# Expert layer of a four-layer network: the two halves of a weight slot waited for, released and fetched apart

## The reference, cut to what matters

```
h = concatenate([pooled.transpose(1, 0, 2), ones])         # 64 experts, 4 rows, 128 + 1
h = gelu(einsum('ebd,edh->ebh', h, weight1))               # 128 (+1) -> 512
h = concatenate([h, ones])
out = einsum('ebh,eho->ebo', h, weight2)                   # 512 (+1) -> 128
```

## Time and profile before

| | |
|---|---|
| median of 3 runs | 3849.9 us (3847.41 to 3853.53) |
| the profiled execution's own time | 3838.93 us |
| its span (first to last instruction) | 3837.2 us |
| mean granted TensorE clock | 0.894 |
| instructions | 82407 |
| busy: PE, DVE, ACT, POOL | 81%, 78%, 68%, 63% of the span |
| the expert loop, 3231.06 to 3326.25 us of the span | 95.2 us, 2.5% of the span |

### The profile page before, as it was taken

One profiled execution on the slowest core, in us unless ns is written; L12 is line 12 of the kernel. 1 busy time (PEld: TensorE's weight loads), 2 busy tenths in 40 slices (PEclk: granted clock), 3 DMA queues, 4 the chain that ended last, 5 costly groups with the idle time before them and its releaser, 6 DMA issues. The chain is left out here.

```text
span 3837.2 us, 82407 instructions
## 1 busy us (share of the span) xinstructions
PE 3117.9 (81%) x29120; PEld 2153.4 (56%) x29152; DVE 2983.9 (78%) x5876; ACT 2603.1 (68%) x5243; POOL 2413.1 (63%) x2896
## 2 busy tenths in 40 slices
PE   7999589999999999999987676788848856678486
PEld 3776356666666666666665353366636534366355
DVE  3999579999999999999998467399858653278754
ACT  5888489999999999999995310267656362077562
POOL 2899588888889998888884220278755130044850
PEclk8999799999999999999999778777769867789698
DMA  3000100000000000000000523510000014500424
GB/s 94 24 24 26 52 4 13 24 24 24 24 24 24 21 17 22 24 24 24 24 18 20 134 56 113 189 29 23 7 6 1 1 25 149 183 5 1 125 52 127
DMA packets 271007, 172.54 MB, mean 45 GB/s; under 512 B 41648, under 2 KB 249976, under 8 KB 268536
## 3 DMA queue, kind: packets, MB, share of 16 engines
q1 hardware_dynamic: 270600, 167.25, 15.2%
HBM read 116.59 MB, written 50.60 MB: 44 GB/s over the span
## 5 line engine op out<-in xcount | busy, mean ns | idle before, releaser
L1246 DVE TENSOR_TENSOR_SCAN mam_hs<-mam_dA,mam_ps_b 128x1024 f32<-128x1024 f32 x512 | 1141.6, 2270 | 80.7 <-issue 43.8
L1162 ACT ACTIVATE mam_dA<-mam_dt,mam_A 128x496 f32<-128x496 f32 x1024 | 658.6, 710 | 0.4
L1018 PE MATMUL mam_ps_h<-mam_ident,mam_hs 128*128 128x128 f32 x4096 | 549.6, 277 | 60.6 <-ACT mam_hTb L1170 30.1
L1018 PEld LDWEIGHTS mam_ps_h<-mam_ident,mam_hs 128*128 128x128 f32 x4096 | 454.1, 142 | 226.3 <-issue 148.5
L1170 ACT COPY mam_hTb<-mam_ps_h 128x512 f32<-128x512 f32 x768 | 423.8, 588 | 96.5 <-PE mam_ps_h L1018 96.5
L1004 PE MATMUL mam_ps_b<-mam_DB,mam_dtxt 32*128 32x512 f32 x2048 | 292.4, 638 | 77.7 <-DVE mam_hs L1246 73.6
L1031 PEld LDWEIGHTS mam_ps_y<-mam_hTb,mam_WC 128*32 128x32 f32 x8192 | 208.9, 109 | 133.2 <-issue 124.4
L1031 PE MATMUL mam_ps_y<-mam_hTb,mam_WC 128*32 128x128 f32 x8192 | 276.7, 276 | 0.3 <-issue 0.3
L780 POOL TENSOR_TENSOR mam_cv<-mam_cv,mam_tap 128x512 f32<-128x512 f32 x180 | 239.1, 1328 | 14.1
L816 POOL TENSOR_TENSOR mam_WC<-mam_cp,mam_m 128x128 f32<-128x128 f32 x512 | 194.3, 410 | 19.9 <-POOL mam_cv L780 14.8
L1256 DVE COPY mam_hTb<-mam_ps_h 128x512 f32<-128x512 f32 x256 | 174.3, 681 | 37.8 <-PE mam_ps_h L1018 36.0
(11 more groups left out here) (742 smaller groups left out, 8236.1 us busy)
## 6 DMA issues: line engine op xcount, KB each, us to landing
moe_wg<-in_L_ffn_weight SPq DMA_DIRECT2D x32, 1024.0 KB, 8.0
rnn_xr<-x SPq DMA_DIRECT2D x23, 512.0 KB, 6.1
l1y_wh<-mode_weights SPq DMA_DIRECT2D x16, 544.0 KB, 3.7
gat_hg<-in_x SPq DMA_DIRECT2D x16, 512.0 KB, 7.2
h<-gat_out SPq DMA_DIRECT2D x32, 256.0 KB, 2.3
mam_ht<-h SPq DMA_DIRECT2D x128, 64.0 KB, 2.0
mam_hr<-h SPq DMA_DIRECT2D x128, 64.0 KB, 2.0
mam_xt<-in_x SPq DMA_DIRECT2D x128, 64.0 KB, 2.1
```

What stands on the lines that cost most here:

```text
L1018: last = pe.transpose(ps_h[n][:, q * P:(q + 1) * P], hs[:, w % 3, c:c + P], ident[:, :])
L1162: act.activation(dA[:, h, :, n, 1:], dt[:, i % 2, h, :].rearrange("p (q t) -> p q t", q=Q)[:, :, 1:], ACT.Exp, scale=A[:, h, n:n + 1]).the ...
L1246: dve.tensor_tensor_scan(hs[:, w % 3, :], dA[:, h, first:first + 2, :, :].rearrange("p q s t -> p (q s t)"), ps_b[:, 2 * (w % 2):2 * (w % ...
```

## The change

The slot gets two sets of semaphores, `win_a` for first halves and `win_b` for second halves. `weights(i)` is split into `first_weights(i)` and `second_weights(i)`. `hidden(i)` waits for `win_a` alone; `output(i)` has a wait for `win_b` in front. From group 4 on, the first half of group i is issued once `hidden(i - 4)` is done (`hid`), and the second half of group i once `output(i - 4)` is done (`out_done`) as before; SP's stream issues them in the order first 4, first 5, first 6, second 4, first 7, second 5, and so on up to first 15, second 13, second 14, second 15. The transfers themselves are the same 32, of the same sizes; there are four semaphores more.

```
-            def weights(i):
-                wa, wb = expert_weights(i)
-                sp.dma_start(wa, w1v[i][0:P]).then_inc(win[i % 4], 16)
-                sp.dma_start(wb..., w2v[i]...).then_inc(win[i % 4], 16)
+            def first_weights(i):
+                sp.dma_start(expert_weights(i)[0], w1v[i][0:P]).then_inc(win_a[i % 4], 16)
+            def second_weights(i):
+                sp.dma_start(expert_weights(i)[1]..., w2v[i]...).then_inc(win_b[i % 4], 16)
...
-            for i in range(4, NG):
-                sp.wait_ge(out_done, i - 3)
-                weights(i)
+            for i in range(4, NG + 2):
+                if i < NG:
+                    sp.wait_ge(hid, i - 3)
+                    first_weights(i)
+                if i >= 6:
+                    sp.wait_ge(out_done, i - 5)
+                    second_weights(i - 2)
...
             def hidden(i):
-                pe.wait_ge(win[i % 4], 32 * (i // 4 + 1))
+                pe.wait_ge(win_a[i % 4], 16 * (i // 4 + 1))
...
             def output(i):
+                pe.wait_ge(win_b[i % 4], 16 * (i // 4 + 1))
                 pe.wait_ge(h_ready, i + 1)
```

More of the change, by code:

```diff
@@ L3290, in routed_experts @@
             "added", "dch", "pch"))
-        win = [s.sem(f"win{j}") for j in range(4)]
+        win_a, win_b = ([s.sem(f"{n}{j}") for j in range(4)] for n in ("win_a", "win_b"))
         block = ctx.enter_context(nc.Block())
@@ L3310, in _ @@
                 sp.dma_start(gb[j * E:(j + 1) * E, :], gate_b.unsqueeze(1)).then_inc(loaded, 16)
-            def weights(i):
-                wa, wb = expert_weights(i)
-                sp.dma_start(wa, w1v[i][0:P]).then_inc(win[i % 4], 16)
-                sp.dma_start(wb.rearrange("p j k o -> p j (k o)"),
-                             w2v[i][:, 0:HID, :].rearrange("j (p k) o -> p j (k o)", k=HC)).then_inc(win[i % 4], 16)
-            weights(0)
+            def first_weights(i):
+                sp.dma_start(expert_weights(i)[0], w1v[i][0:P]).then_inc(win_a[i % 4], 16)
+            def second_weights(i):
+                sp.dma_start(expert_weights(i)[1].rearrange("p j k o -> p j (k o)"),
+                             w2v[i][:, 0:HID, :].rearrange("j (p k) o -> p j (k o)", k=HC)).then_inc(win_b[i % 4], 16)
+            first_weights(0)
+            second_weights(0)
             sp.dma_start(b1[:, :, :], w1[:, P, :].rearrange("e (p k) -> p e k", k=HC)).then_inc(b1_ready, 16)
@@ L3322, in _ @@
             sp.wait_ge(l_done, UNITS)
-            weights(1)
+            first_weights(1)
+            second_weights(1)
             sp.wait_ge(wt_ready, 8)
-            weights(2)
-            weights(3)
-            for i in range(4, NG):
-                sp.wait_ge(out_done, i - 3)
-                weights(i)
+            for i in (2, 3):
+                first_weights(i)
+                second_weights(i)
+            for i in range(4, NG + 2):
+                if i < NG:
+                    sp.wait_ge(hid, i - 3)
+                    first_weights(i)
+                if i >= 6:
+                    sp.wait_ge(out_done, i - 5)
+                    second_weights(i - 2)
             sp.wait_ge(eos_ready, 4)
```

## The result

The changed kernel took 3824.2 us (median of 5 runs, 3810.0 to 3836.5) against 3852.7 for the kernel before (5 runs, 3847.4 to 3854.4); the ratio is 0.9936, interval 0.9918 to 0.9955. The forecast was 3833.7, range 3824 to 3842, so the result lies at its fast edge, 0.2 us inside. Two more measurements gave 0.9924 (0.9906 to 0.9943) and 0.9939 (0.9919 to 0.9958).

What follows compares the result with a forecast made beforehand. The prediction took weight transfers, issued too late to keep the queue filled, to bound the expert loop. Start 4.2, tail 3.4 and holes 8.7 made 16.3 us, less 0.1 for semaphores: 3849.9 - 16.2 = 3833.7 us, range 3824 to 3842.

Steps and rivals of the forecast that it cites:

- The number: Whole expert loop: 16.3 us shorter, from an earlier start, a shorter tail, and the end of holes in the stream.
- What bounds the loop, and why there are holes: Expert loop: weight transfers bound it; slots are released too late, so the queue runs dry about every second group.
- Release order: SP's issues in the loop: both halves go out four turns ahead, 7 MiB queued, so the holes go.
- Start: First issue for group 4: at about 3232.2 instead of 3236.41, 4.2 us earlier.
- The stream: 24 weight transfers in the loop: landing interval 3.05 us per MiB, bounds 2.80 and 3.25, last landing at 3307.9.
- Rival 1, the faster stream,: Loop's transfers: 403 GB/s, 2.60 us per MiB, as lagging engines hold back no others; gain 26.6 us, 3823, chance 0.08.
- likeliest case: Whole change: one stream without holes at 3.05 us per MiB, 3833.7 us, own range 3828 to 3838, chance 0.75.
- Tail: Loop's end after the last landing: only the last second products left, 2.04 us instead of 5.4.
- New waits on PE: Second products wait for their second half: no cost while PE's 4.87 us turn beats two transfers' 6.1.
- Semaphores: Clears at the layer's end: four more semaphores, one more clear per engine, between 0 and 0.2 us, taken as 0.1.
- From stage to whole: Whole kernel: the stage's saving comes off the median in full, 3849.9 - 16.2 = 3833.7 us.
- Rivals 2 to 4: Loop's stream: holes stay, 3842, chance 0.05; deep queue streams slower, 3842, chance 0.08; slower than before, 3858, chance 0.04.

Runs made afterwards that it cites:

- e3: Kernel before with whole slots and one semaphore per slot, PE doing first products last in each turn: loop 82.6 us, ratio 0.9968.
- e4: Changed kernel, with SP letting at most two transfers be on the way from group 4 on: loop 79.1 us, ratio 0.9983.
- e7: Changed kernel without fetching second halves from group 4 on, second products using what the slots hold: loop 43.0 us, one run.
- e1: Kernel before with only the waits for halves apart, both halves still issued together after second products: loop 81.1 us, ratio 0.9958.
- e2: Changed kernel's release and issue order, but first products wait for both halves as in the kernel before: loop 84.7 us, ratio 0.9961.
- e5: Changed kernel, with SP letting at most four transfers be on the way from group 4 on: loop 71.3 us, one run.
- e6: Changed kernel with a fifth slot, group 4 fetched behind group 3 without a wait: loop 66.3 us, ratio 0.9918.
- e8: Changed kernel with five slots and a sixth place for first halves, group 4 and first half 5 fetched early: loop 63.2 us, ratio 0.9929.
- e9: The changed kernel measured again, unaltered, against the kernel before: loop 71.3 us, ratio 0.9939.

## Why the prediction was right, and where it was off

*The number.* The gain of the stage was forecast at 16.3 us and came out at 23.9, so the mechanism was right and its size half as much again. That the total still lies in the range, by 0.2 us, is partly luck: the two repetitions have medians of 3820.1 and 3818.3, under its lower end of 3824, beside kernels before that were also faster (3847.5 and 3845.6).

*What bounds the loop, and why there are holes.* Right. e3 reaches the full rate with whole slots, by keeping more queued; e4 loses it again when only two transfers may be on the way; and e7 shows that at a granted clock of 1.00 nothing else needs more than 43 us.

*Release order.* Right in its effect: with four turns of lead the stream has no holes. Neither part of the change is enough by itself: the waits apart give 14.1 us of the 23.9 (e1), the release apart 10.5 (e2). It was more than needed: four transfers on the way do as well (e5). The queue holds fewer than the 7 MiB counted, since SP is held in its issues (14.4 us to land at 2.76 us each makes 5.2 on the way); this cost nothing, as put.

*Start.* Predicted 1.14 us behind the loop's start, measured 1.1; 4.2 us as said.

*The stream.* Off in size, and this is the term that made the forecast too small. "3.05 us per MiB" was 2.76, under its lower bound of 2.80 too: 23 x 0.29 = 6.7 us of gain missed. It was taken from bursts of four transfers, between which the queue emptied, so that the later ones of a burst had fewer than four on the way. e4 shows what fewer on the way cost: with two the rate is 342 GB/s, 3.07 us per MiB, close to the bursts' mean of 3.00. The stretch at 323 GB/s with busy engines was read as a lasting price of the stream. It was a dip: three transfers were on the way when it began and two from 3286.1 on, and no slice between the ramps of the full stream shows the like. Its halves:
```profile
3285.00:3288.00 3.00, 1.87 (x9) 0.21 (x9) 0.00 (x0) 0.00 (x0) 0.00 (x0) 0.50 1.03 256
3288.00:3291.00 3.00, 2.99 (x40) 2.10 (x36) 0.23 (x1) 0.84 (x2) 0.00 (x0) 0.50 1.01 391
```
What started the dip, and why the share doesn't show it, stays open. The 358 GB/s per core of the Trainium skill, page "DMA: Bandwidth & Descriptors", section "Bandwidth", is not a limit here: the stream holds 387 GB/s for 50 us. The same section gives that figure as the share of a core when both cores of a pair stream, and this program runs on one core. Nor is the 425 GB/s of the Trainium skill, page "HBM Reference", section "Specifications (TRN2)", reached in this trace.

*Rival 1, the faster stream,* had the direction right and gave a mechanism (a lagging engine no longer holds back the others), at 2.60. The truth, 2.76 and 23.9 us of gain, lies between the likeliest case's bound (2.80, 22.1) and the rival (26.6). That the lag of single engines is what a short queue costs is not shown; shown is that the rate grows with what is on the way up to four, and that with two it falls in short dips (e4).

*Tail.* Predicted 2.04, measured 1.1, because the granted clock at the end was 1.00 and not 0.50: 0.9 us. PE now never waits over 1.6 us, and the clock in the loop rose from 0.75 to 0.93. With the stream's 6.7 this closes the sum: 16.3 + 6.7 + 0.9 = 23.9.

*New waits on PE.* Cost nothing, as said: the sum above closes without them, and e7's 43.0 us for the loop shows the room that was left.

*Semaphores.* Loop 23.9 shorter, layer 23.8. The 0.1 us taken fits, but the layer of the change varies by 0.5 us between its three profiles (242.8 to 243.3), so this doesn't show it.

*From stage to whole.* The medians differ by 28.5 us and in the repetition with the most runs of before by 27.4, 4 us more than the layer; the intervals (17 to 36 us) hold 23.8, so the rest can be noise, and no more is shown.

*Rivals 2 to 4.* The holes did not stay (98.6% busy); the deep queue streams faster, not slower.

## What to carry to other kernels

If an engine waits for weights and the transfers run under the rate that a well-filled stream has (here 387 GB/s), count how much is queued behind the piece that it waits for. Then move the release, the wait or the order of the consumer's work until enough is on the way. Each of the three alone raised the rate in the middle of the loop, from 297 GB/s to 344, 368 and 387. For transfers of 1 MiB two on the way were too few and four were enough; three were not tried. An estimate of the least: the first transfer into an empty queue takes 5.6 us from issue to landing and a full stream moves one in 2.71 us, which makes 2.1 on the way.

A transfer's price must be read from a stretch with as much queued as the new kernel will have. The busy share alone doesn't give it: 0.97 went with 342 GB/s, 1.05 with 387, and three microseconds of a dip had 1.03 at 256. Once the stream is full, fewer bytes behind the start help (e6, e8): use the idle stretch ahead of it and what room is left in SBUF.

## What the runs showed that was not expected

- The rate of one stream of 1 MiB transfers in pieces of 2,048 bytes: 342 GB/s with two on the way (share 0.97), 387 with four and with a full queue (share 1.05).
- The layer before the touched one begins at different times in profiles of programs that do not differ up to there: the expert layer's first VectorE instruction stood between 3089.0 us (e9) and 3111.3 us (e6), a spread of 22 us, as large as the gain. The mean granted clock over the whole run was 0.900 and 0.890 in these two. A change of this size is seen far better in the time of its own stage (71.3 us three times) than in the total. e4 shows it too: its layer is 15.5 us shorter than before, which would make a ratio of 0.9960, and the measured one is 0.9983 with an interval that just leaves that out (0.9964 to 1.0002).
